# A recommendation tower on one core: SyncE and ScalarE issue their first transfers behind the landing of the gathers' ids

## What is computed

```python
e = jnp.stack([tbl_0[ids[:, 0]], tbl_1[ids[:, 1]], ..., tbl_25[ids[:, 25]]], axis=1)
all_emb = jnp.concatenate([bottom[:, None, :], e], axis=1)      # (512, 27, 128)
gram = jnp.einsum('bfd,bgd->bfg', all_emb, all_emb)
z = gram[:, TRIU_I, TRIU_J]                                     # upper triangle, no diagonal
h = jnp.concatenate([z, bottom], axis=1)
h = jnp.maximum(h @ W_top1 + b_top1, 0.0)                       # 512 wide
h = jnp.maximum(h @ W_top2 + b_top2, 0.0)                       # 256 wide
return h @ W_top3
```

## Time and profile before

| | us |
|---|---|
| median of 3 runs | 126.03 |
| lowest and highest | 124.89 and 126.24 |
| span of the profiled execution, first to last instruction | 126.5 |
| PE, DVE, ACT, POOL busy in it | 91.8, 80.7, 81.8, 75.5 |

### The profile page before, as it was taken

The page is one execution under the profiler, slowest core; times in us unless marked ns, Lnnn a source line. Parts: engine busy times, 40 slices in busy tenths (PEclk is TensorE's granted clock), DMA queues, the critical chain, the costliest instruction groups (busy, mean ns, idle before and its releaser), DMA issues. The chain is left out here.

```text
span 126.5 us, 3473 instructions
## 1 busy us (share of the span) xinstructions
PE 91.8 (73%) x1395; PEld 73.5 (58%) x1395; DVE 80.7 (64%) x182; ACT 81.8 (65%) x146; POOL 75.5 (60%) x76
## 2 busy tenths in 40 slices
PE   0069889975999969973620864968989897449992
PEld 0048567754788748752510753747776785449971
DVE  1099968996998895465949004896598606983012
ACT  6072999999599699784510592985499525981130
POOL 2078788888789779787777778878777700010000
PEclk9999999999599999997685599599999999995999
DMA  2999997996739993682222222212122200000000
GB/s 67 239 258 228 227 235 158 222 226 188 185 71 241 241 270 69 190 289 51 60 60 55 60 53 62 53 42 67 47 67 62 53 21 5 8 19 0 0 0 1
DMA packets 7001, 14.08 MB, mean 111 GB/s; under 512 B 2027, under 2 KB 2676, under 8 KB 6985
## 3 DMA queue, kind: packets, MB, share of 16 engines
q1 hardware_dynamic: 4632, 9.11, 28.2%
q0 software_dynamic: 2208, 4.48, 14.6%
q10 hardware_dynamic: 144, 0.26, 0.7%
HBM read 13.71 MB, written 0.00 MB: 108 GB/s over the span
## 5 line engine op out<-in xcount | busy, mean ns | idle before, releaser
L313 POOL DMA_INDIRECT emb<-tbl,idx x68 | 74.2, 1091 | 25.3 <-issue 20.4
L720 PE MATMUL pG<-onehot,tab_hi 125*128 125x512 f32 x72 | 21.8, 443 | 10.3 <-ACT tab_hi L473 7.6
L720 PEld LDWEIGHTS pG<-onehot,tab_hi 125*128 125x128 f32 x72 | 14.4, 208 | 15.0 <-ACT tab_hi L473 7.6
L388 DVE TENSOR_SCALAR onehot<-hot 125x512 fp32r<-125x512 int32 x59 | 22.3, 445 | 0.5 <-PE pG L724 0.2
L611 PE MATMUL pT<-ident,emb 128*128 128x128 f32 x68 | 11.4, 297 | 11.5 <-DMA emb<-tbl,idx 11.1
L724 PE MATMUL pG<-onehot,tab_lo 125*128 125x512 f32 x72 | 18.8, 406 | 0.0
L623 PE MATMUL pG<-embT 128*26 128x26 f32 x1024 | 13.5, 199 | 6.7 <-issue 4.9
L461 ACT COPY embT<-pT 128x512 f32<-128x512 f32 (+1 forms) x10 | 10.7, 1065 | 10.9 <-PE pT L611 10.8
L623 PEld LDWEIGHTS pG<-embT 128*26 128x26 f32 x1024 | 11.6, 112 | 9.8 <-issue 7.2
L611 PEld LDWEIGHTS pT<-ident,emb 128*128 128x128 f32 x68 | 8.7, 152 | 13.9 <-DMA emb<-tbl,idx 12.3
L329 DVE COPY embT<-pT 128x512 f32<-128x512 f32 (+1 forms) x10 | 10.3, 1030 | 9.5 <-PE pT L611 9.5
(11 more groups left out here) (69 smaller groups left out, 111.2 us busy)
## 6 DMA issues: line engine op xcount, KB each, us to landing
tab<-tbl SPq DMA_DIRECT2D x8, 448.0 KB
hot<-hot_ids SPq DMA_DIRECT2D x8, 256.0 KB, 4.7
tab<-w SPq DMA_DIRECT2D x7, 256.0 KB, 3.5
emb<-tbl,idx POOLq DMA_INDIRECT x68, 4.1
tab<-tbl SPq DMA_DIRECT2D x9, 52.0 KB
tab<-tbl SPq DMA_DIRECT2D x2, 224.0 KB, 5.6
hot<-hot_ids ACTq DMA_DIRECT2D x1, 256.0 KB, 5.2
bot<-bottom SPq DMA_DIRECT2D x1, 256.0 KB, 6.1
```

Source lines behind the costliest of these rows:

```text
L313: nc.gpsimd.indirect_dma_start(out=emb[:, t % 2, g - LOOKED - 1, :], out_offset=None, in_=tables[f], in_offset=bass.IndirectOffsetOnAxis(a ...
L388: nc.vector.tensor_scalar(hot_rows(i, k), hot[0:VP, i % RING, :], float(k), None, ALU.is_equal).then_inc(s_hotv, 1)
L720: nc.tensor.matmul(pG[i % 2][:, 0, :], tab_hi[:, i % 2, k, :], hot_rows(i, k), start=(k == 0), stop=False)
```

## The change

SP waits for the landing of the ids (`s_ids`, 16) behind the ids' own transfer and ahead of the first table's; ACT waits for it ahead of its first `hot` transfer. Nothing else is changed, and POOL's own wait stays.

```diff
             sp.dma_start(idx[:, :], ids.rearrange("(p t) f -> p (t f)", t=TILES)).then_inc(s_ids, 16)
 
+            sp.wait_ge(s_ids, 16)
             load_table(0, 0, VP_MAIN, 0, VK // 2, s_tab[0])
             load_table(0, VP_MAIN, VP, 0, VK, s_tab[0])
             load_table(0, 0, VP_MAIN, VK // 2, VK, s_tab0_rest)
...
+            act.wait_ge(s_ids, 16)
             act.dma_start(hot[:, 0, :], hot_ids[0:1, :].broadcast_to([128, B])).then_inc(s_hotids[0], 16)
             act.wait_ge(s_ones, 1)
             nc.scalar.copy(prod[:, :, :], ones[:, :].unsqueeze(1).broadcast_to([128, KTILES, 128])).then_inc(s_prod1, 1)
```

## The result

The changed kernel takes 125.03 us (median of 20 executions, 122.89 to 127.84); the kernel before, run beside it, 126.88 us (20 executions, 124.89 to 128.79). The ratio is 0.9856 with a 95% interval of 0.9808 to 0.9904, so 1.4% or about 1.8 us faster. Forecast were 122.8 against 126.03, which is 3.2 us. The direction was right and the gain little more than half of what I said.

The account below looks back on a forecast made before the run. POOL's gather chain was taken to pace the kernel up to PE's wait for gather 42, with 56.7 us fixed behind it. Ids landing sooner start gathers 3.2 us earlier: 126.03 - 3.2 = 122.8 us, range 121.5 to 125.1.

Parts of the forecast that it names:

- What bounds the kernel: POOL's chain of 68 gathers paces the kernel up to 69.80 us; behind that a chain through PE, ACT, DVE and moves.
- T: Point where PE goes on after its wait for gather 42, second group of tile 2; predicted to move from 69.80 to 66.6.
- The gathers' pace: On POOL, from first gather to gather 42: losses beside DVE's work stay the same, change zero, plus or minus 0.8 us.
- The ids' landing: At the start, on SP's queue: the 52 KB of ids land in 2.2 us instead of 5.4, bounded by 1.4 and 3.5.
- What was queued behind the waits: SP's tables and ACT's hot row: first lookup 1.8 to 2.2 us later, at no cost, with 4.7 us to spare.
- the wait at 29.98: PE's 2.04 us wait for gathers 9 to 12 inside the lookups; predicted to be gone or short.
- ids slow by themselves: Rival: SP's queue starts slowly, not crowded out; gain only 0.9 to 1.25 us, time near 125.0; chance 0.16.
- The slower rival: Lookups become the bound with PE at the half clock; 3.3 us slower, 129.3 us; chance 0.06.
- 3.2 us earlier: On POOL at the start: first gather at 3.23 instead of 6.43 us.
- the whole 3.2 us reach the end: The 56.7 us of work from PE's wait for gather 42 to the end stay as long; span 126.5 to 123.3.
- T early and the end not: Sign named ahead: if PE's wait for gather 42 ends early but the kernel does not, the work behind it has changed.
- part of the gain is taken back: Rival: two more gathers meet a subtraction, or PE gets the half clock one stretch more; 1.4 us back, 124.2; chance 0.16.

Follow-up runs that it names:

- single profiles: Four profiles each of the kernel before and the changed kernel, no edit, not chosen by their time; average span 125.53 us before, 123.23 changed.
- late_gathers: The changed kernel with POOL's first gather also waiting for ACT's first hot row; 130.05 us, 1.0297 of the kernel before.
- act_only: Of the two new waits only ACT's is kept, SP issues its tables at once; 0.976 of the kernel before (median 123.75 us), run again 0.983 (124.27 us).
- sp_only: Of the two new waits only SP's is kept, ACT issues its hot row at once; 0.9944 of the kernel before.

## Why the prediction was right or wrong

**What bounds the kernel** was right. The gathers' chain paces the kernel up to T, T is gather 42 in every profile of both kernels, and moving the chain's start moves T by as much: -2.89 against -2.99 us in the single profiles, and `late_gathers` moves it in the other direction. **The gathers' pace**, taken as unchanged, was right on average (61.73 and 61.63 us from the first gather to T); single executions of before spread from 60.9 to 63.4, more than the 0.8 us allowed for.

**The ids' landing** was right in kind and 0.45 us too slow in size: I took 2.2 us, it was 1.75, between the 1.4 of the out transfer and the 1.9 of the 20 KB move.

**What was queued behind the waits** cost nothing, as worked out: PE still waits for gathers ahead of T. The first lookup started 1.1 us later instead of 1.8 to 2.2, and in the two first profiles the lookups' last matmuls ended at 50.6 instead of 52.7, since the wait at 29.98 and the half clock behind it were gone. The late end of 52.7 was a trait of the first profile of before: in the single profiles the lookups end at 50.3 us before and at 50.9 after, on average over four each, 0.6 us later. The Trainium skill's rule to issue early and wait late ("DMA: Bandwidth & Descriptors", section "Rules for kernel authors") does not decide here: the held transfers had time to spare, and the one that gained had none.

**The rival "ids slow by themselves"** fell: 1.75 us. Its premise, that SP's queue started slowly on its own, misread: with the hot row held, the same queue moved 177 packets by 2.6 us. The Trainium skill, "DMA: Bandwidth & Descriptors", section "Queues, rings and completion order", says that each engine works off the transfers of one queue in their order, and `act_only` agrees: SP's tables right behind the ids leave them at 1.8 us. With the hot row in flight as well this doesn't cover what was measured, 4.4 to 5.4 us with the tables behind the ids and 3.3 without (`sp_only`, one profile). The Trainium skill's same section also has an engine take turns between queues, and the prediction, from the earlier trace rows, put 0.9 us on the hot row by it. The trace doesn't agree: it cost 1.5 to 1.6 (`sp_only`, 3.3 against 1.75), and together with the tables 2.7 to 3.7. **The slower rival** fell as well: in the first profile of the changed kernel the lookups, from 8.67 to 50.61, ran at a granted clock of 1.00.

**Where it failed**, in two terms of the sum.

The first is the base. I wrote, ahead of the prediction and in it, that the profiled execution stood 0.5 us above the median of the runs, and so set a span against times. In every execution with both on record the time is 1.8 us more than the span, so the profile of before was an execution of about 126.5 + 1.8 = 128.3 us, near the top of its kernel's spread. Its first gather at 6.43 was the latest of six; in the single profiles it is 5.69. From 5.69 to my 3.23 the step "3.2 us earlier" would have been 2.5 us; since the ids also landed earlier than I thought, it measured 2.9. That it came so near to 3.2 is luck: two errors of opposite sign. The base of the sum, 126.03, was low besides, a median of three runs; twenty gave 126.88, and 0.85 us of the distance between 122.8 and 125.03 is that.

The second is the step "the whole 3.2 us reach the end", by a block of 56.7 us behind T. That block was one of the three shortest of six in the table: in other executions of the same kernel the same work takes up to 60.6 us. In the single profiles 0.7 us of the 3.0 at T are lost behind it. The whole is then 2.3 us by the single profiles, 2.0 by the medians of all executions (127.05 in 85 of before, 125.04 in 38 of the changed kernel), 1.85 by the first comparison. Whether the 0.7 is a cost of the change or the draw of eight executions stays open, and so does its cause. The prediction had named this sign, T early and the end not. I had the half clock in the case "part of the gain is taken back", 1.8 us faster, with a chance of 0.16; the difference came out nearest to that case. The time itself, 125.03, lies at the 125.0 of the rival that fell, which is chance.

## What to carry to other kernels

A small transfer that a long chain waits for should have the queues to itself until it lands, if what it holds back has time to spare; here one 256 KB broadcast on the other queue cost it 1.5 us alone and about 3 us together with the transfers behind it in its own queue, which cost it nothing once the broadcast was held. Hold back the one that hurts first, and measure whether a second hold adds anything; here it brought no earlier landing. Before a gain is put on a median, ask whether the profiled execution is a typical one, comparing span with span and time with time, and whether the work behind the moved point had a good or a bad clock in it.

## What the runs showed of the hardware that was not expected

- A transfer on the other queue took most of the engines from one issued at the same time: with the hot row (a broadcast of 2 KB to 128 partitions) in flight, SP's queue moved 25 packets from 0.7 to 2.6 us and ACT's 49, without it SP's queue moved 177. The bytes of all together were nearly the same, 0.11 and 0.12 MB. Whether a transfer that is no broadcast would do the same was not tried.
- SP's tables behind the ids in the same queue cost the ids nothing alone (1.8 us with the tables, 1.75 without), but with the hot row in flight as well the ids took 4.4 to 5.4 us (six profiles of the kernel before) instead of 3.3 (one profile of `sp_only`).
- One kernel's work of 953 matmuls behind T took between 56.3 and 60.6 us from execution to execution, with PE busy for 43.0 us at a granted clock of 0.92 and for 47.7 at 0.81.
